# Expert gates with the heads innermost, and first-pass scores issued ahead of second-pass work

## The chip, the cores and the metric

The kernel runs on one core of a Trainium2 chip. The metric is the time of one execution on the device in microseconds, as the median of several runs. Each engine (TensorE, VectorE, ScalarE, GpSimd, SyncE) runs its own queue of instructions in order, and the kernel orders them against each other with semaphores.

## The reference

A stream x of shape (8, 512, 128) goes through four residual blocks: attention A, a mixture F, attention B, and the same F again. All are computed on a layer-normalised x.

```python
x = x + attn_a(layernorm(x))      # 16 heads of 8, rotary, causal softmax
x = x + ffn(layernorm(x))
x = x + attn_b(layernorm(x))      # the same shape, other weights and rotary table
x = x + ffn(layernorm(x))

def ffn(x):                       # H = 8 heads of 64, E = 5 experts, 2 chosen
    gl_v = (x @ Ws).reshape(b, t, h, e)
    wv = topk_mask(gl_v, 2) * sigmoid(gl_v)
    v = einsum('bthe,btek->bhtk', wv, einsum('btd,edk->btek', x, Wv))
    attn = softmax(q k^T * scale) @ v            # not causal, 512 x 512 per head
    mask_o = topk_mask((x @ Wd).reshape(b, t, h, e), 2)
    return einsum('bthe,bthk,ekd->btd', mask_o, attn, Wo)
```

What matters here: per token there are two sets of 8 x 5 gate logits. For each head the two largest of the five experts are kept, once with a sigmoid weight (for the values) and once as a plain mask (for the output).

## The kernel before

The work is 16 units (two rounds of 8 batch entries), each an attention block followed by a mixture block. The units are pipelined over iterations j of one long loop: iteration j prepares attention for unit j (`a_prep`), runs attention of unit j-1 (`a`) and prepares its mixture (`f_prep`), runs the mixture of unit j-2 (`f`) and ends that of unit j-3 (`f_end`). There are 19 iterations, and in iterations 3 to 15 all of this is active.

Each iteration has eight slots, 0 to 3 for the four head groups of attention and 4 to 7 for the four head pairs of the mixture, and each slot has ten steps b. Every engine walks the same grid of (slot, step) in its own queue, and the order inside a step is written out by hand.

For each head group there are two passes over the scores. `pass1` (L374) computes scores into one of three PSUM banks S1a to S1c, only so that VectorE finds the row maxima (`maxima`, L831) and, in the mixture, ScalarE takes the exponentials (`exps_f`, L677, into Pq). It runs two slots ahead: slots 2 to 5 hold the first pass of the mixture (L405, at even steps b = 0 to 6, two banks each), slots 6, 7, 0, 1 that of attention (L395 and L397, every step). `pass2` (L408) fills S2a and S2b: scores transposed again for attention (L423, slots 0 to 3), or transposes of Pq for the mixture (L429, slots 4 to 7). ScalarE moves them to PT (`exps`, L669 and L673), GpSimd masks them in attention (L1045), and `values` (L436, L455 and L464) multiplies PT of the slot before with the values into the bank Y. ScalarE copies Y to ySB at step 8 (L729) and TensorE transposes it in step 0 of the next slot (L490).

On TensorE (L598 on) each step issues pass2, then pass1, then values at odd steps, then what else stands in that step: the transposes of Z in step 9 of slot 1 (L582), the output projection of the mixture (L594), the gates (`f_gates`, L560) at steps 5 and 6 of slot 6, the mixture's Q/K projections (L557).

pass1 waits for `s1_free`, which is the reading of the bank three back: by VectorE's maximum in attention, by ScalarE's exponential in the mixture. Since the mixture's pass1 fills two banks at once, at step b it waits for the exponential of bank b-2. pass2 waits for `exps_done` of two banks back, and in the mixture for the exponentials of its own bank. ScalarE does in each step first `exps_f` of bank b-1 and then `exps` of bank b.

The choosing of experts is on VectorE. ScalarE copies the 80 gate logits of each of four token tiles from PSUM to `gate` (L717) in the order (tile, 16 = 8 + 8 heads, expert). `f_compare` (L884; L890 and L893) compares, for each expert e, its logit with those of the others, and writes 0 or 1 into `cmp_` in bfloat16, with the expert that does the beating innermost; nine instructions in steps 7 and 8 of slot 6. `f_count` (L899, L904) sums the innermost axis twice, half of the heads each, in step 9 of slot 6 and step 0 of slot 7: the number of experts that beat this one. `f_sigmoid` (L908) makes the sigmoid in slot 7, steps 1, 2 and 4, and the third step (L918) multiplies with (count < 1.5). `f_pick` (L923, L926) makes the output mask in step 5 of slot 1 of the next iteration. The value products (`f_value_product`, L930, L939) use wv_s from step 8 of slot 1 on, with GpSimd adding them up (L1069). `f_mix_weights` (L944) multiplies the mask with the reciprocal softmax sum into wz in step 1 of slot 6, and `f_mix` (L953, L965) multiplies y with wz, in steps 1 and 3 of slots 6, 7, 0 and 1, with GpSimd adding into Z (L1078) one step later.

## Time and profile before

| | |
|---|---|
| median of 3 runs | 2178.54 us (2177.8 to 2180.32) |
| the profiled execution | 2177.41 us, of which the span from first to last instruction is 2175.7 us |
| TensorE matmul busy | 1890.0 us (87%), 11328 instructions |
| VectorE busy | 1634.7 us (75%), 2950 instructions |
| ScalarE busy | 1278.2 us (59%), 2803 instructions |
| GpSimd busy | 1047.6 us (48%), 1124 instructions |
| mean granted TensorE clock | 0.947 of full speed |

A busy TensorE is a modelled figure, since matmuls are pipelined. Idle time is shown with its releaser: what ended the wait. The longest waits in total are GpSimd's for ScalarE's PT and for VectorE's products, and ScalarE's for the mixture's maxima; they say little, as these engines are not full. In the profile a slot is found by the transposes of ySB (L490), which stand in its step 0.

### The profile page before, as it was taken

The page shows a single profiled execution, that of the slowest core. Times are in us where ns is not written, and L with a number is a line of the kernel's source. Part 1 is how long each engine was busy: PE and PEld are TensorE (multiplying, and loading weights), DVE is VectorE, ACT ScalarE, POOL GpSimd, SP SyncE. Part 2 cuts the span into 40 slices and gives each one's busy share as a digit, 9 for nine tenths or more (in the row PEclk, how much of TensorE's full clock was granted, in tenths as well). Part 3 has the DMA queues.
Part 4 walks back from the last instruction along what each step waited for, and adds up shares of the span by engine and source line. Part 5 has one row for each costly group of instructions (what it writes and reads, how often), then busy time and mean ns, then how long its engine had stood idle before and what let it go on. Part 6 is the DMA issues. An engine that isn't in the chain of part 4 may idle for free.

```text
span 2175.7 us, 32651 instructions
## 1 busy us (share of the span) xinstructions
PE 1890.0 (87%) x11328; PEld 913.3 (42%) x11328; DVE 1634.7 (75%) x2950; ACT 1278.2 (59%) x2803; POOL 1047.6 (48%) x1124
## 2 busy tenths in 40 slices
PE   1658998999899999989999998999999899998775
PEld 0323544435354443535444353544435354443333
DVE  4548787978778797877879787787978788686561
ACT  0326657575665757566565756657575666657451
POOL 1215365463636556363655636365463646544433
PEclk8879999999999999999999999999999999999977
DMA  3221212020121202012120201212021121200000
GB/s 95 43 34 31 34 41 34 28 36 18 38 31 41 35 28 39 19 36 29 40 35 28 42 26 29 31 35 35 28 42 33 24 29 35 35 6 23 1 10 5
DMA packets 87617, 68.71 MB, mean 32 GB/s; under 512 B 10720, under 2 KB 83104, under 8 KB 87328
## 3 DMA queue, kind: packets, MB, share of 16 engines
q1 hardware_dynamic: 87456, 66.62, 16.3%
q8 instruction: 94, 1.54, 0.3%
q14 instruction: 67, 0.55, 0.1%
HBM read 32.51 MB, written 10.49 MB: 20 GB/s over the span
## 4 chain that ended last, share of the span: by engine, by line
PE 56%; DVE 30%; ACT 7%; issue 3%; DMA 2%; POOL 1%; SPq 0%; POOLq 0%; DVEq 0%; PEldq 0%; ACTq 0%
PE Y L464 8%; DVE nmaxF L849 5%; DVE nmaxA L844 5%; PE S1c L405 4%; PE S1b L405 4%; ACT Pq L684 4%; DVE ztmp L965 4%; PE S2a L429 4%; PE S2b L429 4%; PE M L594 3%; PE S1a L405 3%; PE Y L455 3%; PE M L557 3%; PE M L490 2%; DVE rotated L890 2%
## 5 line engine op out<-in xcount | busy, mean ns | idle before, releaser
L1078 POOL TENSOR_TENSOR Z<-Z,ztmp 128x1280 f32<-128x1280 f32 x112 | 324.5, 2898 | 353.3 <-DVE ztmp L965 351.2
L1045 POOL TENSOR_SCALAR_AFFINE_SELECT PT<-PT 128x256 f32<-128x256 f32 (+1 forms) x640 | 253.5, 406 | 372.8 <-ACT PT L669 368.9
L1069 POOL TENSOR_TENSOR Vf<-Vf,ztmp 128x512 f32<-128x512 f32 x256 | 349.6, 1366 | 146.8 <-DVE ztmp L939 138.3
L464 PE MATMUL Y<-PT,Vf 128*64 128x512 f32 x1024 | 274.8, 617 | 0.0
L669 ACT ACTIVATE PT<-S2a 128x512 f32<-128x512 f32 x320 | 191.3, 598 | 120.0 <-PE S2a L423 119.4
L405 PE MATMUL S1a<-Kf,Qf 64*128 64x512 f32 x352 | 217.5, 700 | 6.6 <-ACT Pq L684 4.6
L939 DVE TENSOR_TENSOR ztmp<-xv,wv_s 128x512 f32<-128x512 f32 x256 | 217.2, 848 | 2.8 <-POOL Z L1078 2.8
L405 PE MATMUL S1c<-Kf,Qf 64*128 64x512 f32 x352 | 207.9, 672 | 12.1 <-ACT Pq L684 10.8
L673 ACT ACTIVATE PT<-S2a 128x512 f32<-128x512 f32 x256 | 153.4, 599 | 89.2 <-PE S2a L429 89.0
L669 ACT ACTIVATE PT<-S2b 128x512 f32<-128x512 f32 x320 | 191.5, 598 | 16.3 <-PE S2b L423 15.7
L405 PE MATMUL S1b<-Kf,Qf 64*128 64x512 f32 x320 | 194.5, 690 | 6.5 <-ACT Pq L684 6.5
L849 DVE TENSOR_REDUCE nmaxF<-S1c 128x1 f32<-128x512 f32 x176 | 120.5, 685 | 93.9 <-PE S1a L405 93.9
L684 ACT ACTIVATE Pq<-S1c,nmaxF 128x512 f32<-128x512 f32 x176 | 121.6, 691 | 116.6 <-DVE nmaxF L849 116.6
L455 PE MATMUL Y<-PT,Vs 128*9 128x512 f32 (+3 forms) x2048 | 188.0, 441 | 0.0
L429 PE MATMUL S2a<-ident,Pq 128*128 128x128 f32 x1024 | 166.3, 285 | 24.0 <-ACT PT L669 24.0
L849 DVE TENSOR_REDUCE nmaxF<-S1a 128x1 f32<-128x512 f32 x176 | 120.4, 684 | 84.6 <-PE S1b L405 84.4
L965 DVE TENSOR_TENSOR ztmp<-M,wz 128x1280 f32<-128x1280 f32 x112 | 165.6, 1481 | 23.9 <-PE M L490 21.7
L429 PEld LDWEIGHTS S2a<-ident,Pq 128*128 128x128 f32 x1024 | 112.3, 142 | 161.6 <-ACT PT L673 88.3
L673 ACT ACTIVATE PT<-S2b 128x512 f32<-128x512 f32 x256 | 152.2, 595 | 30.0 <-PE S2b L429 27.6
L844 DVE TENSOR_REDUCE nmaxA<-S1b 128x1 f32<-128x128 f32 (+2 forms) x272 | 126.0, 492 | 54.5 <-PE S1b L397 54.5
L684 ACT ACTIVATE Pq<-S1a,nmaxF 128x512 f32<-128x512 f32 x176 | 121.0, 687 | 74.6 <-DVE nmaxF L849 74.5
L429 PE MATMUL S2b<-ident,Pq 128*128 128x128 f32 x1024 | 162.5, 283 | 0.0
(109 smaller groups left out, 3905.2 us busy)
## 6 DMA issues: line engine op xcount, KB each, us to landing
Qs<-parts SPq DMA_DIRECT2D x96, 128.0 KB
Ks<-parts SPq DMA_DIRECT2D x96, 128.0 KB
tab_s<-in_tab SPq DMA_DIRECT2D x16, 512.0 KB, 4.4
xr<-out_x SPq DMA_DIRECT2D x32, 256.0 KB, 2.9
out_x<-res SPq DMA_DIRECT2D x32, 256.0 KB, 2.2
wa_s<-in_wa SPq DMA_DIRECT2D x16, 320.0 KB, 3.1
xl<-out_x SPq DMA_DIRECT2D x16, 256.0 KB, 2.9
out_x<-in_x SPq DMA_DIRECT2D x8, 256.0 KB, 4.4
```

The source lines that it names most:

```text
L405: nc.tensor.matmul(S1[(n - 1 + h) % len(S1)][:, :], Qf[own, pair, qt * P:qt * P + P], Kf[own, pair, :], start=True, stop=True).then_inc(s1 ...
L429: last = nc.tensor.transpose(t[:, kt * P:kt * P + P], Pq[:, slot % 2, b, kt * P:kt * P + P], ident[:, :])
L455: last = nc.tensor.matmul(Y[32 * h:32 * h + DA + 1, kt * P:T], Vs[:, kt, GA * group + h, :], PT[:, group % 2, b, col:col + T - kt * P], st ...
L464: last = nc.tensor.matmul(Y[DF * h:DF * h + DF, :], Vf[:, kt, GF * (group - SA) + h, :], PT[:, group % 2, NT * h + kt, :], start=(kt == 0) ...
L669: nc.scalar.activation(PT[:, slot % 2, b, :], t[:, :], ACT.Exp, scale=SCALE_A).then_inc(exps_done.sem, 1)
L673: nc.scalar.activation(PT[:, slot % 2, NT * h:NT * h + NT, qt * P:qt * P + P], t[:, :].rearrange("p (k q) -> p k q", q=P), ACT.Copy).then_ ...
L684: nc.scalar.activation(Pq[:, g % 2, b, :], S1[(n - 1) % len(S1)][:, :], ACT.Exp, bias=nmaxF[:, GF * g + h, qt:qt + 1], accum_out=denF[:, G ...
L849: nc.vector.tensor_reduce(nmaxF[:, GF * (group - SA) + h, qt:qt + 1], t[:, :], AX.X, ALU.max, negate=True).then_inc(maxF_ready.sem, 1)
L965: nc.vector.tensor_tensor(ztmp[:, hh % 2, :, :, :] if hh else Z[:, :, :, :], y[:, :, h:h + 1, :].broadcast_to([P, NT, E, DF]), wz[:, :, hh ...
L1045: last = nc.gpsimd.affine_select(out=v, in_=v, compare_op=ALU.is_ge, fill=0.0, base=0, pattern=pattern, channel_multiplier=-1)
L1069: nc.gpsimd.tensor_tensor(Vf[:, i, :, :], Vf[:, i, :, :], vtmp[:, n % VBUF, :, :], ALU.add).then_inc(v_acc.sem, 1)
L1078: nc.gpsimd.tensor_tensor(Z[:, :, :, :], Z[:, :, :, :], ztmp[:, hh % 2, :, :, :], ALU.add).then_inc(z_acc.sem, 1)
```

## The change

Two things are changed. First, every array of the choosing has the experts outermost and the heads innermost. The columns of the gate weights are reordered on the host, `gate`, `beaten_by`, `wv_s` and `wz` become (expert, tile, head), `denF` and `recF` become (tile, head), and `cmp_` becomes (the beating expert, the beaten one, tile and head). The comparisons are then contiguous, and `f_count` reads its summed axis with a step of 320 bfloat16 elements. `f_pick` is removed with its array: `f_mix_weights` compares the count with 1.5 and multiplies in one scalar_tensor_tensor. The third sigmoid step goes from step 4 to step 9 of slot 7. Second, TensorE issues pass1 ahead of pass2 in each step.

```diff
@@ -125,20 +125,19 @@
         Kf = sb("Kf", [P, PAIRS, T])
 
         Pq = sb("Pq", [P, 2, GF * NT, T])
-        gate = sb("gate", [P, NT, 2 * HF, E])
+        gate = sb("gate", [P, E, NT, 2 * HF])
         xv = sb("xv", [P, NT, NX])
-        beaten_by = sb("beaten_by", [P, NT, 2 * HF, E], BF)
-        pick = sb("pick", [P, NT, HF, E])
-        wv_s = sb("wv_s", [P, NT, HF, E])
+        beaten_by = sb("beaten_by", [P, E, NT, 2 * HF], BF)
+        wv_s = sb("wv_s", [P, E, NT, HF])
         Vf = sb("Vf", [P, NT, HF, DF])
         nmaxF = sb("nmaxF", [P, HF, NT])
         rotated = sb("rotated", [P, 2, T])
         rot, rot2 = rotated[:, 0, :], rotated[:, 1, :]
         cmp_ = rotated[:, :, :].rearrange("p a t -> p (a t)").bitcast(BF)[:, 0:NT * 2 * HF * E * E].rearrange(
-            "p (g a b) -> p g a b", a=E, b=E)
-        denF = sb("denF", [P, HF, NT])
-        recF = sb("recF", [P, HF, NT])
-        wz = sb("wz", [P, NT, HF, E])
+            "p (b a g) -> p b a g", a=E, b=E)
+        denF = sb("denF", [P, NT, HF])
+        recF = sb("recF", [P, NT, HF])
+        wz = sb("wz", [P, E, NT, HF])
         Z = sb("Z", [P, NT, E, DF])
         ztmp = sb("ztmp", [P, 2, NT, E, DF])
         maskf = ztmp[:, 0, 0, 0:2, :].rearrange("p a b -> p (a b)")
@@ -234,7 +233,7 @@
         outA_chain = Signal("outA_chain", 1)
         maxA_chain = Signal("maxA_chain", SA)
         normA_chain = Signal("normA_chain", SA)
-        pick_chain = Signal("pick_chain", 7)
+        pick_chain = Signal("pick_chain", 6)
         mix_chain = Signal("mix_chain", 2)
 
         def bank(use):
@@ -597,10 +596,10 @@
 
                 for slot in range(NS):
                     for b in range(STEPS):
+                        if b < N_BANKS[(slot + AHEAD) % NS]:
+                            pass1(slot, b)
                         if b < N_BANKS[slot]:
                             pass2(slot, b)
-                        if b < N_BANKS[(slot + AHEAD) % NS]:
-                            pass1(slot, b)
                         if b % 2 == 1 and b < 2 * NT:
                             values(slot, b // 2)
                         at = (slot, b)
@@ -683,7 +682,7 @@
                         act.wait_ge(mix_chain.sem, mix_chain.at(j, 1, 3))
                     nc.scalar.activation(Pq[:, g % 2, b, :], S1[(n - 1) % len(S1)][:, :], ACT.Exp,
                                          bias=nmaxF[:, GF * g + h, qt:qt + 1],
-                                         accum_out=denF[:, GF * g + h, qt:qt + 1]).then_inc(expF_done.sem, 1)
+                                         accum_out=denF[:, qt, GF * g + h:GF * g + h + 1]).then_inc(expF_done.sem, 1)
 
                 def rows(group):
                     if not (a_prep if group == 0 else a):
@@ -714,7 +713,7 @@
                     if i == 0:
                         act.wait_ge(v_mult.sem, v_mult.at(j, v_mult.per, 2))
                     act.wait_ge(*filled(j, use))
-                    nc.scalar.activation(gate[:, i, :, :].rearrange("p g e -> p (g e)"), bank(use)[:, 0:NG], ACT.Copy)
+                    nc.scalar.activation(gate[:, :, i, :], bank(use)[:, 0:NG].rearrange("p (e g) -> p e g", e=E), ACT.Copy)
                     nc.scalar.activation(xv[:, i, :], bank(use)[:, NG:NG + NX], ACT.Copy).then_inc(is_free(use), 1)
 
                 for slot in range(NS):
@@ -761,8 +760,8 @@
                         if at == (6, 7) and f_prep:
                             act.wait_ge(*drained(j, "F gate2"))
                             act.wait_ge(*drained(j, "F gate3"))
-                            nc.scalar.activation(wv_s[:, :, :, :].rearrange("p t h e -> p t (h e)"),
-                                                 gate[:, :, 0:HF, :].rearrange("p t h e -> p t (h e)"),
+                            nc.scalar.activation(wv_s[:, :, :, :].rearrange("p e t h -> p (e t) h"),
+                                                 gate[:, :, :, 0:HF].rearrange("p e t h -> p (e t) h"),
                                                  ACT.Exp, scale=-1.0).then_inc(sig_e.sem, 1)
 
             for j in range(LAST):
@@ -885,28 +884,28 @@
                     if e == 0:
                         dve.wait_ge(*drained(j, "F gate2"))
                         dve.wait_ge(*drained(j, "F gate3"))
-                    gl = gate[:, :, :, :].rearrange("p t g e -> p (t g) e")
+                    gl = gate[:, :, :, :].rearrange("p e t g -> p e (t g)")
                     n_gl = NT * 2 * HF
-                    last = nc.vector.tensor_tensor(cmp_[:, :, 0:e + 1, e], gl[:, :, e:e + 1].broadcast_to([P, n_gl, e + 1]),
-                                                   gl[:, :, 0:e + 1], ALU.is_gt)
+                    last = nc.vector.tensor_tensor(cmp_[:, e, 0:e + 1, :], gl[:, e:e + 1, :].broadcast_to([P, e + 1, n_gl]),
+                                                   gl[:, 0:e + 1, :], ALU.is_gt)
                     if e < E - 1:
-                        last = nc.vector.tensor_tensor(cmp_[:, :, e + 1:E, e],
-                                                       gl[:, :, e:e + 1].broadcast_to([P, n_gl, E - 1 - e]),
-                                                       gl[:, :, e + 1:E], ALU.is_ge)
+                        last = nc.vector.tensor_tensor(cmp_[:, e, e + 1:E, :],
+                                                       gl[:, e:e + 1, :].broadcast_to([P, E - 1 - e, n_gl]),
+                                                       gl[:, e + 1:E, :], ALU.is_ge)
                     else:
                         last.then_inc(pick_chain.sem, 1)
 
                 def f_count(half):
                     dve.wait_ge(pick_chain.sem, pick_chain.at(j, 1, 1))
-                    n = NT * HF
-                    by = beaten_by[:, :, :, :].rearrange("p t g e -> p (t g) e")
+                    n = E * NT * HF
+                    by = beaten_by[:, :, :, :].rearrange("p e t g -> p (e t g)")
+                    beats = cmp_[:, :, :, :].rearrange("p b a g -> p (a g) b")
                     with nc.allow_low_precision(reason="counts of at most 4 are exact in bfloat16"):
-                        nc.vector.tensor_reduce(by[:, n * half:n * half + n, :], cmp_[:, n * half:n * half + n, :, :],
+                        nc.vector.tensor_reduce(by[:, n * half:n * half + n], beats[:, n * half:n * half + n, :],
                                                 AX.X, ALU.add).then_inc(pick_chain.sem, 1)
 
-
                 def f_sigmoid(step):
-                    wv2 = wv_s[:, :, :, :].rearrange("p t h e -> p (t h e)")
+                    wv2 = wv_s[:, :, :, :].rearrange("p e t h -> p (e t h)")
                     if step == 0:
                         dve.wait_ge(sig_e.sem, sig_e.at(j, 1, 1))
                         nc.vector.tensor_scalar(wv2, wv2, 1.0, None, ALU.add).then_inc(pick_chain.sem, 1)
@@ -915,21 +914,13 @@
                         nc.vector.reciprocal(wv2, wv2).then_inc(pick_chain.sem, 1)
                     if step == 2:
                         dve.wait_ge(pick_chain.sem, pick_chain.at(j, 5, 1))
-                        nc.vector.scalar_tensor_tensor(wv_s[:, :, :, :].rearrange("p t h e -> p t (h e)"),
-                                                       beaten_by[:, :, 0:HF, :].rearrange("p t h e -> p t (h e)"), 1.5,
-                                                       wv_s[:, :, :, :].rearrange("p t h e -> p t (h e)"),
+                        wv3 = wv_s[:, :, :, :].rearrange("p e t h -> p (e t) h")
+                        nc.vector.scalar_tensor_tensor(wv3, beaten_by[:, :, :, 0:HF].rearrange("p e t h -> p (e t) h"), 1.5, wv3,
                                                        ALU.is_lt, ALU.mult).then_inc(pick_chain.sem, 1)
-
-                def f_pick():
-
-                    dve.wait_ge(pick_chain.sem, pick_chain.at(j, 6, 2))
-                    nc.vector.tensor_scalar(pick[:, :, :, :].rearrange("p t h e -> p t (h e)"),
-                                            beaten_by[:, :, HF:2 * HF, :].rearrange("p t h e -> p t (h e)"), 1.5, None,
-                                            ALU.is_lt).then_inc(pick_chain.sem, 1)
 
                 def f_value_product(i, e):
                     if i == 0 and e == 0:
-                        dve.wait_ge(pick_chain.sem, pick_chain.at(j, 7, 2))
+                        dve.wait_ge(pick_chain.sem, pick_chain.at(j, 6, 2))
                         dve.wait_ge(y_filled.sem, y_filled.at(j, 1))
                     if i == 0 and e == 1:
                         dve.wait_ge(z_acc.sem, z_acc.at(j, HF - 1, 3))
@@ -939,16 +930,18 @@
                     nc.vector.tensor_tensor(
                         vtmp[:, n % VBUF, :, :] if e else Vf[:, i, :, :],
                         xv[:, i:i + 1, e * DF:(e + 1) * DF].broadcast_to([P, HF, DF]),
-                        wv_s[:, i, :, e:e + 1].broadcast_to([P, HF, DF]), ALU.mult).then_inc(v_mult.sem, 1)
+                        wv_s[:, e, i, :].unsqueeze(2).broadcast_to([P, HF, DF]), ALU.mult).then_inc(v_mult.sem, 1)
 
                 def f_mix_weights():
 
                     dve.wait_ge(expF_done.sem, expF_done.at(j, expF_done.per, 2))
                     nc.vector.reciprocal(recF[:, :, :], denF[:, :, :]).then_inc(mix_chain.sem, 1)
                     dve.wait_ge(mix_chain.sem, mix_chain.at(j, 1, 2))
-                    nc.vector.tensor_tensor(wz[:, :, :, :], pick[:, :, :, :],
-                                            recF[:, :, :].rearrange("p h t -> p t h").unsqueeze(3).broadcast_to([P, NT, HF, E]),
-                                            ALU.mult).then_inc(mix_chain.sem, 1)
+                    dve.wait_ge(pick_chain.sem, pick_chain.at(j, 3, 2))
+                    nc.vector.scalar_tensor_tensor(
+                        wz[:, :, :, :].rearrange("p e t h -> p e (t h)"), beaten_by[:, :, :, HF:2 * HF], 1.5,
+                        recF[:, :, :].rearrange("p t h -> p (t h)").unsqueeze(1).broadcast_to([P, E, NT * HF]),
+                        ALU.is_lt, ALU.mult).then_inc(mix_chain.sem, 1)
 
                 def f_mix(g, h, lag):
 
@@ -964,7 +957,7 @@
                         dve.wait_ge(z_acc.sem, z_acc.at(j, hh - 2, lag))
                     nc.vector.tensor_tensor(ztmp[:, hh % 2, :, :, :] if hh else Z[:, :, :, :],
                                             y[:, :, h:h + 1, :].broadcast_to([P, NT, E, DF]),
-                                            wz[:, :, hh, :].unsqueeze(3).broadcast_to([P, NT, E, DF]),
+                                            wz[:, :, :, hh].rearrange("p e t -> p t e").unsqueeze(3).broadcast_to([P, NT, E, DF]),
                                             ALU.mult).then_inc(z_mult.sem, 1)
                     if h == GF - 1:
                         dve.wait_ge(z_mult.sem, z_mult.at(j, GF * g + GF, lag))
@@ -1010,10 +1003,8 @@
                                 f_compare(e)
                         if at in ((6, 9), (7, 0)) and f_prep:
                             f_count(slot - 6)
-                        if at in ((7, 1), (7, 2), (7, 4)) and f_prep:
-                            f_sigmoid((1, 2, 4).index(b))
-                        if at == (1, 5) and f:
-                            f_pick()
+                        if at in ((7, 1), (7, 2), (7, 9)) and f_prep:
+                            f_sigmoid((1, 2, 9).index(b))
                         if at in V_STEPS and f:
                             f_value_product(*divmod(V_STEPS.index(at), E))
                         if at == (2, 1) and f_end:
@@ -1144,6 +1135,7 @@
     Wv, Wo = np.asarray(L0_ffn_Wv), np.asarray(L0_ffn_Wo)
     E, _, DH = Wv.shape
     HE = L0_ffn_Ws.shape[1]
+    gates = np.concatenate([np.asarray(w).reshape(C, HE // E, E) for w in (L0_ffn_Ws, L0_ffn_Wd)], 1)
     arrays = {
         "x": x,
         "wa": np.stack([a[0], b[0]]),
@@ -1153,7 +1145,7 @@
         "bp": np.stack([a[4], b[4]]),
         "tab": np.stack(tabs).astype(np.float32),
         "wqk": np.concatenate([np.asarray(L0_ffn_Wq), np.asarray(L0_ffn_Wk)], 1),
-        "wgv": np.concatenate([np.asarray(L0_ffn_Ws), np.asarray(L0_ffn_Wd), Wv.transpose(1, 0, 2).reshape(C, E * DH)], 1),
+        "wgv": np.concatenate([gates.transpose(0, 2, 1).reshape(C, 2 * HE), Wv.transpose(1, 0, 2).reshape(C, E * DH)], 1),
         "wo": Wo.reshape(E * DH, C),
         "ident": np.eye(128, dtype=np.float32),
         "mask": np.triu(np.full((128, 128), -1e30, np.float32), 1),
```

## Rows read from the trace of the kernel before

**Rows 1.** windows: span us, busy us (instructions) of PE, PEld, DVE, ACT, POOL, clock, DMA

```profile
1096.00:1222.00 126.00, 116.27 (x709) 56.47 (x708) 101.45 (x185) 79.52 (x175) 65.57 (x71) 0.97 0.16 33
```

**Rows 2.** VectorE groups by shape: count | busy us, mean ns | idle before

```profile
L844 DVE TENSOR_REDUCE nmaxA<-S1a 128x1 f32<-128x512 f32 x96 | 65.2, 680 | 3.1 <-PE S1a L397 3.1
L904 DVE TENSOR_REDUCE beaten_by<-rotated 128x160 bf16<-128x800 bf16 x32 | 31.1, 974 | 0.0
...
L844 DVE TENSOR_REDUCE nmaxA<-S1b 128x1 f32<-128x128 f32 x96 | 26.7, 278 | 0.0
L890 DVE TENSOR_TENSOR rotated<-gate 128x320 bf16<-128x320 f32 x16 | 20.5, 1281 | 0.0
L890 DVE TENSOR_TENSOR rotated<-gate 128x64 bf16<-128x64 f32 x16 | 7.1, 442 | 5.4 <-ACT xv L718 5.4
```

**Rows 3.** VectorE groups by line, shapes together

```profile
L890 DVE TENSOR_TENSOR rotated<-gate 128x64 bf16<-128x64 f32 (+4 forms) x80 | 69.6, 886 | 5.4 <-ACT xv L718 5.4
L893 DVE TENSOR_TENSOR rotated<-gate 128x256 bf16<-128x256 f32 (+1 forms) x64 | 54.5, 851 | 0.0
```

**Rows 4.** one line each: duration in ns as least/median/most

```profile
L918 DVE SCALAR_TENSOR_TENSOR wv_s<-beaten_by,wv_s x16: 319/2395/2405, 163.6 to 2036.1; 128x160 f32<-128x160 bf16 x16
L926 DVE TENSOR_SCALAR pick<-beaten_by x16: 234/2646/2659, 182.4 to 2051.2; 128x160 f32<-128x160 bf16 x16
```

**Rows 5.** TensorE timeline, slot 1: start us, duration us, what [idle before]

```profile
1186.59 0.39 PE L395 MATMUL S1c<-Ks,Qs 96*128 96x512 bf16 x1 [0.74 <-DVE nmaxA L839]
...
1190.41 0.28 PE L395 MATMUL S1b<-Ks,Qs 96*128 96x256 bf16 x1 [2.15 <-DVE nmaxA L844]
...
1190.76 2.69 PE L582 MATMUL M<-ident,Z 128*128 128x128 f32 x12
```

**Rows 6.** VectorE timeline, slot 1

```profile
1187.04 2.64 DVE L926 TENSOR_SCALAR pick<-beaten_by 128x160 f32<-128x160 bf16 x1
```

**Rows 7.** GpSimd timeline, slot 1

```profile
1186.71 2.88 POOL L1078 TENSOR_TENSOR Z<-Z,ztmp 128x1280 f32<-128x1280 f32 x1
```

**Rows 8.** windows, columns as in rows 1: behind slots 1 and 3, and slot 5

```profile
1191.00:1193.00 2.00, 2.00 (x11) 1.62 (x10) 1.93 (x10) 1.07 (x2) 1.17 (x2) 0.50 0.00 0
1193.00:1195.50 2.50, 2.50 (x11) 1.04 (x9) 2.50 (x7) 1.21 (x3) 1.28 (x3) 0.73 0.04 10
...
1228.00:1232.00 4.00, 4.00 (x18) 2.00 (x20) 2.02 (x5) 2.41 (x6) 2.08 (x4) 0.57 0.57 64
...
1241.00:1245.00 4.00, 2.78 (x24) 1.57 (x16) 4.00 (x6) 3.45 (x8) 3.23 (x3) 1.00 0.57 63
```

**Rows 9.** TensorE timeline, start of slot 3, inside it, start of slot 4

```profile
1211.99 0.38 PE L423 MATMUL S2a<-Qs,Ks 98*128 98x512 bf16 x1 [0.85 <-ACT PT L669]
...
1218.23 0.69 PE L405 MATMUL S1c<-Kf,Qf 64*128 64x512 f32 x1 [0.23 <-ACT Pq L684]
...
1219.29 1.98 PE L515 MATMUL M<-xnT,wa_s 128*128 128x512 f32 x4
...
1225.51 0.39 PE L423 MATMUL S2b<-Qs,Ks 98*128 98x256 bf16 x2 [1.09 <-ACT PT L669]
...
1227.56 0.66 PE L429 MATMUL S2a<-ident,Pq 128*128 128x128 f32 x4 [1.66 <-ACT PT L669]
```

**Rows 10.** ScalarE timeline, end of slot 3

```profile
1226.24 0.69 ACT L684 ACTIVATE Pq<-S1c,nmaxF 128x512 f32<-128x512 f32 x1 [0.79 <-DVE nmaxF L849]
...
1226.92 0.59 ACT L669 ACTIVATE PT<-S2a 128x512 f32<-128x512 f32 x1
```

**Rows 11.** TensorE timeline, starts of slots 5 and 6, and slot 7

```profile
1241.97 0.69 PE L405 MATMUL S1c<-Kf,Qf 64*128 64x512 f32 x1 [0.18 <-ACT Pq L684]
...
1244.13 0.66 PE L490 MATMUL M<-ident,ySB 128*128 128x128 f32 x4 [1.04 <-ACT ySB L729]
...
1259.91 0.66 PE L490 MATMUL M<-ident,ySB 128*128 128x128 f32 x4 [0.77 <-ACT ySB L729]
...
1288.22 1.98 PE L557 MATMUL M<-xnT,wqk_s 128*128 128x512 f32 x4 [0.73 <-DVEq L971]
```


## The prediction

> **What bounds the kernel now.** I read the busy time by stretches first. An iteration takes 126.15 us (the same stall stands at 1186.59 and 126.15 us later), and in 126 us of it TensorE is busy for 116.3 us and VectorE for 101.5 [rows 1]. TensorE is nearly full, so an edit is worth what it takes out of TensorE's 9.8 us of gaps, and what TensorE runs faster where a gap no longer lowers its clock. (The chain that ended last runs over TensorE and, in slots 6 to 1, over VectorE.) Then I walked TensorE's timeline through one iteration and noted each gap with its releaser: 0.74 and 2.15 us in slot 1 [rows 5], 0.85 before slot 3, 0.23 and 1.09 in slot 3, 1.66 before slot 4 [rows 9], 0.18 and 1.04 at the start of slot 5, 0.77 in slot 6, 0.73 in slot 7 [rows 11]. They add up to 9.4 of the 9.8 us. The clock comes last: granted 1.00 nearly everywhere, but 0.50 behind the slot 1 gaps and 0.57 behind the slot 3 gaps, while it stayed at 1.00 around the single gap of 1.04 us [rows 8]. Half speed is 1.2 of 2.4 GHz.
>
> **The change, part by part.** I go by iteration, and count the 15 in which attention and mixture both run (2 to 16).
>
> *The comparisons (f_compare).* Now 124.1 us in 16 iterations, 7.76 us each [rows 3]. They write and read across heads: from 64 to 320 elements the time grows by 839 ns, 3.3 ns an element, and 64 elements alone cost 442 ns [rows 2]. A contiguous reduction goes from 278 to 680 ns between 128 and 512 elements: 1.05 ns an element and 144 ns fixed [rows 2]. The nine new comparisons are contiguous: 1600 elements x 1.05 + 9 x 144 = 2.98 us, 4.8 us less on VectorE.
>
> *The counts (f_count).* Two reductions of 800 elements, 974 ns each [rows 2], whose innermost axis was contiguous and now steps by 640 bytes. The trace has no strided reduction. Lower end: 974 ns. Upper end: every element at the price of a comparison whose streams are all strided, (442 - 144) / 64 = 4.7 ns, so 800 x 4.7 + 144 = 3.9 us. I take 2.0 us, because only one stream of three is strided: +2.05 us for both, so choosing is 2.75 us shorter.
>
> The Trainium skill (SBUF, State Buffer; SBUF: two separate sides) speaks against this edit: lines are of 16 bytes, and each access that crosses to a new one pays. By it each count element would pay where five shared about one line; this trace shows the price in the comparisons only. What it would make of the time is the third rival below.
>
> *The pick (f_pick).* Removed. Its 16 instructions last 234 ns at best and 2646 ns at the median [rows 4]. In slot 1 it starts at 1187.04 and runs to 1189.68 [rows 6], and GpSimd's addition into Z runs from 1186.71 to 1189.59 [rows 7]: it ends when that ends. Its comparison moves into the wz instruction, where no GpSimd work runs, and I cost that at nothing (one 160-element instruction for another). Without it the sixth-step maxima of slot 1 start 2.6 us earlier, and TensorE doesn't wait 2.15 us at 1190.41. What is late next is GpSimd: the transposes of Z, at 1190.76, need the addition that ends at 1189.59 [rows 5, 7]. So the gain is 1190.76 - 1189.6 = 1.15 us, not 2.15, and a gap of about 1 us stays. The clock: at 0.50 for 2 us, and the next 2.5 us (0.73) still partly low [rows 8]; 1.0 + 0.7 us of work lost. One gap of 1 us is like the one that cost no clock, so I count 1.5 us back.
>
> The Trainium skill (SBUF, State Buffer; Who interferes with whom) gives the reason: VectorE and GpSimd share one port pair, and the later one is held until the other ends. The trace agrees (2646 against 234 ns).
>
> *The last sigmoid step.* 319 ns at best, 2395 at the median [rows 4], for the same reason; it moves from step 4 to step 9 of slot 7, behind five more maxima and away from the addition. Its readers, the value products, come in the last steps of slot 1. This saves 2.0 us of VectorE in slot 7, where TensorE only waits 0.73 us for VectorE, to free the bank for the third Q/K projection [rows 11]. The comparisons alone bring VectorE 2.75 us ahead of that point, so I count 0.7 us for all of slots 6 and 7; the rest is VectorE time that nobody waits for.
>
> *The order on TensorE.* Each step issued second pass, first pass, values, and will issue first pass, second pass, values. No DMA, SP or GpSimd queue is passed; the only thing moved is 1.06 us of F scores (at full clock, 1218.23 to 1219.29, four even steps of each of slots 2 to 5), or 0.3 to 0.4 us of A scores in slots 6 to 1. The two passes wait for different things: the first pass for a score bank that ScalarE's exponentials freed, the second pass for ScalarE's copy of two banks before. At the start of slot 4 TensorE waits 1.66 us for that copy, at 1226.92, which is itself behind the exponential of 1226.24 [rows 9, 10]. The first pass of that step needs only an older bank, so its 1.06 us go into the gap. At the start of slot 3 it fills the 0.85, but then the pass of step 4 comes to an exponential for which it already waits 0.23 us at 1218.23 [rows 9], and now 0.3 us of second pass are queued behind that wait; I let 0.5 of the 0.85 through. Sum 1.55 us. Behind slot 3 the clock is at 0.57 for 4 us, 1.7 us lost [rows 8]. There the gaps before were 1.09 and 1.66, and will be 1.09 and 0.6 with 1.4 us of work between. I leave the clock there as it is in the forecast, and keep the 1.5 us as a case.
>
> At the starts of slots 5 and 6 TensorE waits for ScalarE's copy of Y (1.04 and 0.77 us) [rows 11]; that copy stands behind the last exponential, thus behind the last first pass of the slot, which now comes one F second pass earlier (0.66 us as shown, 0.6 to its successor) [rows 9]. Slot 6: 0.6 us. Slot 5: 0.18 + 0.6, less 0.4 because in slot 4 the loop of first pass 1.06, second pass 0.6, its copy and the next exponential (0.59 and 0.69 [rows 10], some 0.2 more with hand-overs, an estimate) is 3.1 us, slightly more than TensorE's own work there. Left: 0.4 us.
>
> In slots 6 to 1 the first pass waits for VectorE's maxima of three banks before. Where VectorE is late (0.74 us at 1186.59) [rows 5], 0.3 us of second pass is now held behind it; it ends before GpSimd does, and costs nothing. If that cover were gone, 0.3 us an iteration.
>
> **Sum.** 1.15 + 1.5 (clock, slot 1) + 1.55 + 0.4 + 0.6 + 0.7 = 5.9 us a period, 15 x 5.9 = 88.5 us. The profiled execution took 2177.41 us (a span of 2175.7), 1.1 under the median 2178.54, which gives 2088.9 and 2090. The first and last iterations run other limits and I count nothing there.
>
> **Rivals.**
> 1. *Both low-clock stretches go*: 7.4 us a period, 2178.5 - 111 = 2067. For: four fifths of the stretch before slot 4 would be work. Against: the two gaps still add to 1.7 us.
> 2. *Neither goes*: 4.4 us, 2112.
> 3. *The counts by columns cost their upper end.* 3.9 us each is +5.85 on VectorE against the 4.8 saved, so the wait in slot 7 grows by 1.05 instead of losing 0.7: 4.15 us, 62 us, 2116. The rule of the Trainium skill on lines, above, points here.
> 4. *The order buys nothing*, as ScalarE and VectorE recur at their own pace and each early score only waits longer for its bank. Left are 1.15 + 1.5 + 0.7 = 3.35 us, 2128. For it: ScalarE waits for the maxima in these slots, 0.79 us in the row shown [rows 10].
> 5. *Slower.* The first pass blocks the second. In each of the 16 first-pass pairs of slots 2 to 5 TensorE stops for the exponential of two banks before, and the second pass, which could run in that wait, is issued behind it. Then the copies come late, and with them the next exponentials. If one attention second pass, 0.32 us, is lost at each, 5.1 us stand against the 3.35 of rival 4: +1.8 a period, 2205. It decides from 0.21 us a pair. Against it: only one of the pairs of slot 3 waits now, 0.23 us.
> 6. *No effect*: VectorE is only freed where TensorE was full. Against it speaks the slot 1 stall.
>
> **Chances.** Forecast 0.38, rival 1 0.18, rival 2 0.14, rival 3 0.10, rival 4 0.12, rival 5 0.06, rival 6 0.02. About 0.2% (4 us) is what a measurement of this kernel can tell from no change. Faster 0.92, within 0.2% 0.02, slower 0.06. The range runs from under rival 1 to over rival 4: 2055 to 2140.
>
> **What would show it.** No stall over 1.3 us in slot 1, its releaser GpSimd's Z addition and not VectorE; comparisons near 3 us an iteration; counts between 1 and 3.9 us; the last sigmoid step near 0.32 us; first-pass scores ahead of the gap at the start of slots 3 and 4; the copy of Y no longer waited for in slot 6. The forecast is wrong if TensorE's waits for the exponentials in slots 2 to 5 grow over 2 us a period, or if the clock behind slot 1 stays low.

## The result, and the profile after

The changed kernel takes 2077.8 us (median of 6, 2074.39 to 2081.19), the one before 2178.68 in the same comparison (2177.78 to 2180.32): ratio 0.9537, 95% interval 0.9524 to 0.9549. The forecast was 2090 in a range of 2055 to 2140, so sign and range held; the kernel gained 101 us where 88.5 were forecast. The profiled execution took 2074.39 us (span 2072.6). Line numbers (L...) from here on are those of the kernel named; the changed kernel's are 1 to 10 lower than before.

First the window of one iteration (columns as in [rows 1]):

```profile
1081.00:1200.00 119.00, 111.60 (x713) 54.40 (x712) 98.35 (x184) 79.50 (x176) 65.55 (x70) 1.00 0.20 34
```

The clock is 1.00 over the whole iteration (0.97 before), and TensorE is busy for 5 us less than in [rows 1] although it does the same work. Each execution has 13 iterations that are alike (counted from one first transpose of Z to the next). In the changed kernel ten of them keep the full clock, and three have one stretch of 3.4 us at half speed and last 1.4 to 1.6 us longer. Then TensorE's timeline through that iteration, the gaps alone:

```profile
1080.70 0.66 PE L489 MATMUL M<-ident,ySB 128*128 128x128 f32 x4 [0.73 <-ACT ySB L728]
...
1131.55 0.39 PE L394 MATMUL S1c<-Ks,Qs 96*128 96x512 bf16 x1 [0.21 <-DVE nmaxA L838]
1135.10 1.09 PE L581 MATMUL M<-ident,Z 128*128 128x128 f32 x8 [1.32 <-POOL Z L1069]
1136.50 0.63 PE L581 MATMUL M<-ident,Z 128*64 128x128 f32 x4 [0.31 <-ACT parts L659]
...
1146.91 0.69 PE L404 MATMUL S1a<-Kf,Qf 64*128 64x512 f32 x1 [0.34 <-ACT Pq L683]
1157.56 0.69 PE L404 MATMUL S1a<-Kf,Qf 64*128 64x512 f32 x1 [0.31 <-ACT Pq L683]
1161.25 0.69 PE L404 MATMUL S1c<-Kf,Qf 64*128 64x512 f32 x1 [1.26 <-ACT Pq L683]
1168.42 0.39 PE L422 MATMUL S2b<-Qs,Ks 98*128 98x256 bf16 x2 [0.76 <-ACT PT L668]
...
1170.37 0.66 PE L428 MATMUL S2a<-ident,Pq 128*128 128x128 f32 x4 [0.51 <-ACT PT L668]
1176.09 0.69 PE L404 MATMUL S1b<-Kf,Qf 64*128 64x512 f32 x1 [0.16 <-ACT Pq L683]
1179.16 0.69 PE L404 MATMUL S1a<-Kf,Qf 64*128 64x512 f32 x1 [0.37 <-ACT Pq L683]
1182.23 0.69 PE L404 MATMUL S1c<-Kf,Qf 64*128 64x512 f32 x1 [0.58 <-ACT Pq L683]
1184.14 0.66 PE L489 MATMUL M<-ident,ySB 128*128 128x128 f32 x4 [0.19 <-ACT ySB L728]
1199.49 0.66 PE L489 MATMUL M<-ident,ySB 128*128 128x128 f32 x4 [0.73 <-ACT ySB L728]
```

From the first to the last of these is one iteration, 118.79 us against 126.15: 7.4 us less. The gaps shown add to 7.05 us (9.4 before). Slot 1 waits 1.84 us (2.89 in [rows 5]), and the longest of its waits is for GpSimd's addition; the starts of slots 3 and 4 with what lies between, 2.84 (3.83 in [rows 9]); slot 5, 0.77 (1.22), slot 6 as before 0.73, slot 7 nothing [rows 11]. New waits: 0.34 in slot 2, 0.16 and 0.37 in slot 4.

Sorted by what they wait for, the waits of slots 2 to 5 moved more than they shrank. Those for ScalarE's exponentials (Pq) grew from 0.41 us (0.23 + 0.18) to 3.02; those for ScalarE's copies (PT and ySB) fell from 4.64 (0.85 + 1.09 + 1.66 + 1.04) to 1.46. Together that is 0.57 us less.

Behind slots 1 and 3 the clock stays up (the stretches of [rows 8]):

```profile
1135.50:1139.50 4.00, 3.69 (x26) 1.92 (x28) 3.96 (x12) 2.27 (x4) 2.47 (x6) 1.00 0.02 4
1170.50:1174.50 4.00, 3.96 (x28) 1.97 (x29) 3.57 (x7) 3.62 (x9) 3.37 (x5) 1.00 0.57 73
```

VectorE's groups by shape, against [rows 2 to 4]:

```profile
L904 DVE TENSOR_REDUCE beaten_by<-rotated 128x160 bf16<-128x800 bf16 x32 | 49.2, 1539 | 0.0
L889 DVE TENSOR_TENSOR rotated<-gate 128x320 bf16<-128x320 f32 x16 | 7.7, 481 | 0.0
...
L941 DVE SCALAR_TENSOR_TENSOR wz<-beaten_by,recF 128x160 f32<-128x160 bf16 x16 | 5.2, 325 | 0.5
L918 DVE SCALAR_TENSOR_TENSOR wv_s<-beaten_by,wv_s 128x160 f32<-128x160 bf16 x16 | 5.1, 316 | 0.1
...
L889 DVE TENSOR_TENSOR rotated<-gate 128x64 bf16<-128x64 f32 x16 | 3.4, 215 | 6.0 <-ACT xv L717 6.0
```

The nine comparisons sum to 3.01 us an iteration (forecast 2.98, before 7.76), the counts take 1539 ns each (forecast 2000, before 974), the last sigmoid step 316 ns.

### The profile page after: what moved, and what is told of

The parts are those of the page before. It is cut to its first block, busy times and chain, and to the rows that moved or that the text cites. A ratio compares the mean times of both kernels' runs of the same rounds, so it can differ in the third digit from the quotient of the medians.

```text
span 2072.6 us, 32651 instructions
## 1 busy us (share of the span) xinstructions
PE 1816.3 (88%) x11328; PEld 881.0 (43%) x11328; DVE 1580.1 (76%) x2934; ACT 1273.3 (61%) x2803; POOL 1047.0 (51%) x1124
## 4 chain that ended last, share of the span: by engine, by line
PE 64%; DVE 13%; ACT 10%; POOL 6%; DMA 3%; issue 3%; SPq 0%; POOLq 0%; DVEq 0%; ACTq 0%; PEldq 0%
PE Y L463 11%; PE M L556 5%; POOL Z L1069 5%; PE S2a L428 5%; ACT Pq L683 5%; PE S1c L404 5%; PE S2b L428 4%; DVE nmaxF L848 4%; PE M L593 3%; PE S1b L404 3%; PE M L514 3%; PE M L489 3%; DMA Ks<-parts 3%; DVE ztmp L930 3%; PE Y L454 2%
## 5 line engine op out<-in xcount | busy, mean ns | idle before, releaser
L930 DVE TENSOR_TENSOR ztmp<-xv,wv_s 128x512 f32<-128x512 f32 x256 | 238.0, 930 | 2.8 <-POOL Z L1069 2.8
L404 PE MATMUL S1c<-Kf,Qf 64*128 64x512 f32 x352 | 203.6, 659 | 36.2 <-ACT Pq L683 32.2
L404 PE MATMUL S1a<-Kf,Qf 64*128 64x512 f32 x352 | 204.5, 662 | 20.6 <-ACT Pq L683 20.6
L404 PE MATMUL S1b<-Kf,Qf 64*128 64x512 f32 x320 | 182.8, 652 | 9.5 <-ACT Pq L683 9.5
L428 PE MATMUL S2b<-ident,Pq 128*128 128x128 f32 x1024 | 155.3, 274 | 0.0
L848 DVE TENSOR_REDUCE nmaxF<-S1b 128x1 f32<-128x512 f32 x160 | 109.3, 683 | 40.0 <-PE S1c L404 37.9
```

What stands on the lines that cost most here:

```text
L404: nc.tensor.matmul(S1[(n - 1 + h) % len(S1)][:, :], Qf[own, pair, qt * P:qt * P + P], Kf[own, pair, :], start=True, stop=True).then_inc(s1 ...
L428: last = nc.tensor.transpose(t[:, kt * P:kt * P + P], Pq[:, slot % 2, b, kt * P:kt * P + P], ident[:, :])
L848: nc.vector.tensor_reduce(nmaxF[:, GF * (group - SA) + h, qt:qt + 1], t[:, :], AX.X, ALU.max, negate=True).then_inc(maxF_ready.sem, 1)
L930: nc.vector.tensor_tensor(vtmp[:, n % VBUF, :, :] if e else Vf[:, i, :, :], xv[:, i:i + 1, e * DF:(e + 1) * DF].broadcast_to([P, HF, DF]), ...
```

## The experiments

All ran in 3 rounds, each compared with runs of the kernel before on its own chip (2176.3 to 2179.5 us), so that ratios are comparable: changed kernel 0.9537.

### The two parts alone

e1_order_only is the kernel before with the new order; e2_layout_only is the changed kernel with the old order. The edit of e1 (that of e2 is the reverse):

```diff
-                        if b < N_BANKS[slot]:
-                            pass2(slot, b)
                         if b < N_BANKS[(slot + AHEAD) % NS]:
                             pass1(slot, b)
+                        if b < N_BANKS[slot]:
+                            pass2(slot, b)
```

> The kernel before with the first pass issued ahead of the second pass in every step; choosing, pick and sigmoid as before. Theory A (the prediction's sum, terms add): 1.55 + 0.4 + 0.6 us an iteration from the order and 1.5 from the clock behind slot 3, 4.05 x 15 = 61 us, about 2118 us (2140 if the low clock behind slot 3 stays). The 2.15 us stall of slot 1 and the 0.73 us wait in slot 7 stay. Theory B (only VectorE's relief counts; each early score waits longer for its bank): within 5 us of 2178. Theory C (the first pass holds up the second where VectorE is late, which only shows while the pick stands in slot 1): slower than 2178.

> The changed kernel with the second pass issued first again: only the heads innermost, no pick, sigmoid step in step 9. Theory A: 1.15 us (slot 1 up to GpSimd's addition) + 1.5 (clock behind slot 1) + 0.7 (slot 7) = 3.35 us x 15 = 50 us, about 2128 us; the gaps of 0.85, 1.09 and 1.66 us around slots 3 and 4 stay with the low clock behind them. Theory B: most of the 101 us, near 2080. If the two parts need each other, the gains of this run and of the order alone add to clearly less than 101 us; theory A says 111 with both clock terms.

Measured: e1 2091.06 us, ratio 0.9608 (0.9589 to 0.9628); e2 2121.14, ratio 0.9743 (0.9725 to 0.9761). The layout alone gained 55 us where 50 were expected; the order alone gained 85 where its theory A had 61. Together they gain 101 us, one by one 85 + 55 = 140, so 39 us are counted twice. By the traces these are, per iteration, 1.0 us of waits in slot 1 (2.89 before, 1.85 in e1, 1.92 in e2, 1.84 with both) and about 2.2 us of low clock: either part alone makes most of the low stretches go away. How the order removes the stall of slot 1 without touching the pick, VectorE's and GpSimd's timelines of e1 in slot 1 show:

```profile
1142.12 0.68 DVE L844 TENSOR_REDUCE nmaxA<-S1a 128x1 f32<-128x512 f32 x1
1142.72 0.28 DVE L926 TENSOR_SCALAR pick<-beaten_by 128x160 f32<-128x160 bf16 x1
1142.92 0.74 DVE L844 TENSOR_REDUCE nmaxA<-S1b 128x1 f32<-128x384 f32 x2
...
1142.87 2.89 POOL L1078 TENSOR_TENSOR Z<-Z,ztmp 128x1280 f32<-128x1280 f32 x1
```

In [rows 6, 7] the pick started 0.33 us behind GpSimd's addition and lasted to its end, 2.64 us. With the scores of each step issued one second pass earlier it starts 0.15 us ahead of the addition and takes 0.28 us. What e1 has against the changed kernel are two short waits for VectorE in slot 7, which stand behind the comparisons and counts:

```profile
1115.08 0.39 PE L395 MATMUL S1b<-Ks,Qs 96*128 96x512 bf16 x1 [0.20 <-DVE nmaxA L844]
1118.19 1.98 PE L557 MATMUL M<-xnT,wqk_s 128*128 128x512 f32 x4 [0.33 <-DVEq L971]
```

An iteration of e1 lasts 119.84 us, 1.05 more than the changed kernel's; the two waits are 0.53 of this. So on top of the order the layout is worth 1.05 us an iteration (forecast 0.7), and on top of the layout the order is worth 0.9743 - 0.9537, 45 us or 3.0 an iteration (forecast 2.55 without the clock behind slot 3, 4.05 with it).

### The pick moved instead of removed

e3_pick_moved is the kernel before with the pick at step 6 of slot 5 (two semaphore waits are moved to suit, not shown):

```diff
-                        if at == (1, 5) and f:
+                        if at == (5, 6) and f:
                             f_pick()
```

> The kernel before with one instruction moved: the pick goes from step 5 of slot 1 to step 6 of slot 5, where GpSimd has nothing to do. Theory A: the pick falls from 2646 to about 234 ns, the slot 1 stall of 2.15 us is replaced by a wait of about 1 us for GpSimd's Z addition, the clock behind it stays at 1.00: 2.65 us x 15 = 40 us, 2139 us. If the clock falls all the same: 1.15 x 15 = 17 us, 2161. Rival (the pick is slow by itself, because of its strided bfloat16 source): it stays near 2.6 us in its new place and the time stays within 10 us of 2178.

2159.34 us, ratio 0.9917 (0.9897 to 0.9938): 18 us, or 1.2 us an iteration, where 2.65 were forecast for this term. (The time is close to the 2161 that was expected if the clock behind slot 1 fell all the same, but that clock didn't fall; the match is luck.) The pick takes 233 ns, TensorE waits for GpSimd in slot 1, and the clock there is whole again. The forecast missed what happened elsewhere. Windows of e3 behind slot 1, behind slot 3 of that iteration, and behind slot 3 of the next:

```profile
1183.00:1187.00 4.00, 3.69 (x25) 1.87 (x27) 3.97 (x12) 2.16 (x4) 2.46 (x6) 1.00 0.02 6
1218.50:1222.50 4.00, 4.00 (x17) 2.01 (x16) 1.41 (x3) 2.35 (x6) 2.27 (x4) 0.57 0.57 68
...
1342.00:1347.00 5.00, 4.78 (x16) 2.79 (x16) 1.59 (x4) 2.92 (x7) 2.73 (x4) 0.50 0.57 74
```

Before, two stretches of 3.4 us ran at half speed in each iteration. In e3 the one behind slot 1 is gone, but the one behind slot 3 is 3.4 and 6.8 us long in turn. So in the mean only 1.7 us of low clock was saved, 0.85 us of time, and not 1.5. The gap fell by less than 1.15 as well: the waits of slot 1 in e3 are 0.74 + 1.07 + 0.31 = 2.12 us against 2.89.

### The pick put back under the addition

e9_order_pick_later is e1 with the pick one step later, where the addition is under way:

```diff
-                        if at == (1, 5) and f:
+                        if at == (1, 6) and f:
                             f_pick()
```

> The kernel with the new order alone (old layout, 2091.06 us), and the old pick of the five smallest moved from step 5 to step 6 of slot 1, where GpSimd's Z addition is under way. Theory A (the strided pick takes 233 to 285 ns when it runs ahead of GpSimd's addition and 2.6 us under it, and then holds up VectorE, then GpSimd and TensorE, as in the kernel before): pick at 2.6 us, the wait of some 1.15 us in slot 1 back, with or without 1.5 us of low clock behind it: 2108 to 2131. Rival B (what made the order alone so good has nothing to do with where the pick lies): 2087 to 2095.

2105.1 us, ratio 0.9662 (0.9648 to 0.9677), 0.86 us an iteration over e1 (120.70 against 119.84). Duration of the pick in ns as least/median/most, and TensorE behind it:

```profile
L926 DVE TENSOR_SCALAR pick<-beaten_by x16: 233/2478/2489, 185.1 to 1976.4; 128x160 f32<-128x160 bf16 x16
...
1152.25 0.66 PE L405 MATMUL S1c<-Kf,Qf 64*128 64x512 f32 x1 [0.81 <-DVE nmaxA L844]
```

So the place of the pick decides its length, as theory A says, but not its price: here 2.5 us of VectorE cost one wait of 0.81 us where theory A had at least 1.15, and the time lies between the two ranges, in neither. The end of the pick is the same each time: 0.10 us behind the end of the addition, whether it starts 0.34 us into it (the kernel before, 2.65 us long), 0.50 (e9, 2.48 us) or 1.53 (the last one of e1, 1.45 us). The Trainium skill (SBUF — State Buffer; SBUF: two separate sides) calls this an exclusive lock on one port pair, held for a whole instruction; 233 against 2478 ns for the same instruction agrees.

### One step of the order alone

e4_step0_only is the changed kernel with the scores first in step 0 of each slot and the second pass first elsewhere:

```diff
-                        if b < N_BANKS[(slot + AHEAD) % NS]:
+                        early = b == 0
+                        if early and b < N_BANKS[(slot + AHEAD) % NS]:
                             pass1(slot, b)
                         if b < N_BANKS[slot]:
                             pass2(slot, b)
+                        if not early and b < N_BANKS[(slot + AHEAD) % NS]:
+                            pass1(slot, b)
```

> The changed kernel with the first pass ahead of the second in step 0 of each slot only, and behind it in all other steps. Theory A: it keeps the filled gaps at the starts of slots 3 and 4 and the clock, and loses the 0.4 + 0.6 us an iteration that the earlier scores gave to the copies of Y at the starts of slots 5 and 6: about 15 us slower than the changed kernel, 2093. Rival: in the changed kernel TensorE waits 2.4 us an iteration for exponentials inside slots 3 and 4 (1.26, 0.15, 0.37, 0.58), with second-pass work queued behind; if that costs more than the earlier scores give, this kernel is faster than the changed one, 2065 or less.

2091.9 us, ratio 0.9606 (0.9587 to 0.9625). Step 0 alone carries two thirds of the order's gain (30 of 45 us). TensorE's timeline and the clock at the start of slot 4:

```profile
1178.20 0.39 PE L422 MATMUL S2b<-Qs,Ks 98*128 98x256 bf16 x2 [1.10 <-ACT PT L671]
1180.25 0.66 PE L428 MATMUL S2a<-ident,Pq 128*128 128x128 f32 x4 [0.60 <-ACT PT L671]
...
1180.50:1184.50 4.00, 4.00 (x29) 1.92 (x28) 3.15 (x5) 3.99 (x10) 3.37 (x5) 1.00 0.57 70
```

The 1.66 us of [rows 9] is 0.60, exactly as worked out, and with it the clock behind slot 3 stays at 1.00 in 10 of the 13 iterations that are alike. With 1.10 + 1.66 us it fell in all 13 of the kernel before and in 10 of e2; with 0.76 + 0.51 in one of the changed kernel and in none of e1. That is the clock term that the forecast left out.

The time of e4 is that of theory A, but not for its reason. It does lose 0.4 us at the start of slot 5 (1.21 us against 0.77), but 0.1 and not 0.6 at slot 6, and inside slots 2 to 4 it waits less; in all its waits are 6.73 us an iteration against 7.05. What makes it slower is something else, which the busy time of whole iterations at full clock shows (e2, e4, the changed kernel):

```profile
1162.37:1283.24 120.87, 112.96 (x709) 54.97 (x709) 96.11 (x184) 79.49 (x175) 65.45 (x71) 1.00 0.19 34
...
1144.59:1264.27 119.68, 112.81 (x708) 54.85 (x709) 96.86 (x184) 79.36 (x175) 65.65 (x71) 1.00 0.19 34
...
1016.31:1135.10 118.79, 111.39 (x708) 54.19 (x709) 98.21 (x184) 79.36 (x175) 65.55 (x71) 1.00 0.17 34
```

For the same matmuls TensorE is busy 1.4 to 1.6 us less when the scores come first in the steps behind step 0 too. The same for ten of the kernels; "own time" is an iteration at full clock less its waits of 0.15 us or more:

| kernel | scores first | iteration us | waits us | own time us | iterations with low clock, of 13 |
|---|---|---|---|---|---|
| before | no | 126.15 (clock low twice) | 9.47 | 113.3 (3.4 taken off for the clock) | 13 |
| e3 | no | 123.97 (clock low once) | 8.71 | 113.6 (1.7 taken off for the clock) | 13 |
| e2 | no | 120.87 | 7.77 | 113.1 | 10 |
| e4 | step 0 | 119.69 | 6.73 | 113.0 | 3 |
| e7 | all but 5 steps | 119.18 | 6.62 | 112.6 | 1 |
| e1 | all | 119.84 | 7.75 | 112.1 | 2 |
| changed | all | 118.79 | 7.05 | 111.7 | 3 |
| e5 | all | 118.30 | 6.57 | 111.7 | 0 |
| e10 | all | 117.44 | 5.71 | 111.7 | 2 |
| e12 | all | 116.90 | 5.19 | 111.7 | 0 |

So of the 3.0 us that the order is worth on top of the layout, 0.7 are waits, 1.4 are TensorE's own time and the rest is clock (10 low stretches against 3). Why the same matmuls take less in the new order was not tried.

### VectorE's time in slots 6 and 7

Two kernels add work into tiles that nobody reads. e8_twice does comparisons and counts a second time, e11_counts_twice the counts:

```diff
+                        nc.vector.tensor_reduce(by2[:, n * half:n * half + n], beats[:, n * half:n * half + n, :],
+                                                AX.X, ALU.add)
                         nc.vector.tensor_reduce(by[:, n * half:n * half + n], beats[:, n * half:n * half + n, :],
                                                 AX.X, ALU.add).then_inc(pick_chain.sem, 1)
...
+                                f_compare(e, cmp2, False)
                                 f_compare(e, cmp_, True)
```

> The changed kernel with the comparisons and the two counts each done a second time into tiles that nobody reads, 3.01 + 3.08 = 6.1 us more of VectorE an iteration in slots 6 and 7. The new layout saves about as much VectorE time there (7.76 + 1.95 before against 3.01 + 3.08 after: 3.6 us). Theory A (what the layout gives on top of the order is VectorE's time in slots 6 and 7, some 1.0 us an iteration, and a wait for VectorE at the start of slot 7 that comes back): the time goes up to that of the kernel with the new order alone or a little over, 2088 to 2105. Rival B (VectorE has room in these slots and what the layout gives lies elsewhere): 2076 to 2082.

> The changed kernel with the two counts alone done a second time into a tile that nobody reads: 3.1 us more of VectorE an iteration. With comparisons and counts doubled (6.1 us more) the time was 2156, and TensorE waited 0.88 + 1.42 + 1.19 + 0.33 = 3.8 us in slot 7 for VectorE's maxima, where it waits for nothing in the changed kernel. Theory A (VectorE has 6.1 - 3.8 = 2.3 us to spare in slots 6 and 7 in the changed kernel, and what goes past it costs its full time): 3.1 - 2.3 = 0.8 us an iteration, time 2086 to 2095; the same sum gives 3.6 - 2.3 = 1.3 us for the old layout's extra work, near to the 1.0 measured. Rival B (the cost grows in proportion from the first microsecond): half of 78 us, time 2113 to 2121.

e8: 2156.39 us, ratio 0.9898 (0.9883 to 0.9913). e11: 2124.48, ratio 0.9759 (0.9732 to 0.9787). Both fell outside both ranges, e11 only 3.5 us above rival B's: 6.1 us of VectorE cost 5.2 us an iteration, and 3.1 us of it cost 3.1, with a few more low stretches in both. TensorE in slot 7 of e11:

```profile
1128.85 0.28 PE L395 MATMUL S1a<-Ks,Qs 96*128 96x256 bf16 x1 [0.69 <-DVE nmaxA L844]
1130.99 0.39 PE L395 MATMUL S1b<-Ks,Qs 96*128 96x512 bf16 x1 [1.20 <-DVE nmaxA L844]
```

A third wait, of 0.33 us, stands at the Q/K projection, as in e1. So there is no common reserve of 2.3 us. At full clock an iteration of e11 lasts 121.53 us, 2.74 over the changed kernel, with 2.2 us of new waits for 3.1 us of VectorE; e8's lasts 123.28, 4.5 over it, with 3.8 us of new waits for 6.1. And a stop costs a little more than its gap: 0.5 us is not in the three new gaps of e11 and 0.7 not in the four of e8, some 0.17 us a stop. The likely reason is that matmuls overlap (the profile starts one of 0.22 us 0.06 us ahead of its successor) and a stop lays the end of the last one open; that was not tried by itself.

The third step of the sigmoid, back at step 4 of slot 7 (e6_sigmoid_back):

```diff
-                        if at in ((7, 1), (7, 2), (7, 9)) and f_prep:
-                            f_sigmoid((1, 2, 9).index(b))
+                        if at in ((7, 1), (7, 2), (7, 4)) and f_prep:
+                            f_sigmoid((1, 2, 4).index(b))
```

> The changed kernel with the third step of the sigmoid (L918) put back from step 9 to step 4 of slot 7, as in the kernel before, where it lies beside a Z addition of GpSimd. Theory A (a strided operation of VectorE beside GpSimd's addition takes 2.4 us instead of 0.32; in slot 7 of the changed kernel it takes what VectorE has to spare there, 2.3 us, so most of it is not seen): L918 at 2.4 us, time 2074 to 2085. Rival B (every microsecond of VectorE in slot 7 is paid): 2.1 us times 15, time 2105 to 2112.

2081.2 us, ratio 0.9558 (0.9531 to 0.9584), not distinct from the changed kernel, with the step at full length:

```profile
L918 DVE SCALAR_TENSOR_TENSOR wv_s<-beaten_by,wv_s x16: 314/2401/2405, 164.0 to 1938.4; 128x160 f32<-128x160 bf16 x16
```

So moving this step gives nothing that can be measured (an iteration at full clock lasts 118.82 us against 118.79): 2.1 us at step 4 are free, where 3.1 us at steps 9 and 0 are not. The gain of the layout on top of the order therefore lies elsewhere. The shorter comparisons are the likely place, as e1's two waits come right behind them; no run takes them apart from the removed pick.

### The waits that are left

e7_hybrid issues the second pass first at five steps of slots 2 to 4, to work inside the waits for ScalarE:

```diff
+                        early = (slot, b) not in ((2, 2), (3, 2), (3, 4), (4, 4), (4, 6))
```

> The changed kernel, but at five steps (second and third step pairs of slots 2 to 4, where TensorE still waits for exponentials or copies behind the scores: 0.34, 0.31, 1.26, 0.76, 0.51 us an iteration) the second pass is issued first again. Theory A (the waits that are left are for the banks of the first pass, and second-pass work done inside them fills them): about 1.8 us an iteration less, 15 times, time 2051 to 2060. Rival B (ScalarE's and VectorE's work comes at its own pace, so a wait filled at one step comes back at the next, and the old order brings its own waits of 0.8 to 1.1 us back): 2078 to 2095.

2080.6 us, ratio 0.9553 (0.9538 to 0.9569): the time is in rival B's range. The 1.26 us of slot 3 came back as waits of 0.81 and 0.28, the 0.58 at the start of slot 5 as 0.76 and its 0.19 as 0.45. In all the waits fell by 0.4 us an iteration, and TensorE's own time grew by 0.8 (table above), which is not what either theory says. Order alone gains nothing more here. The next three kernels, each on top of the one before, take away what ends such a wait last. e5_z_first issues GpSimd's addition ahead of the mask:

```diff
+                        if b in (2, 4) and slot in (0, 1, 6, 7) and (f if slot > 1 else f_end):
+                            f_mix((slot - 2) % NS - SA, b // 2 - 1, 3 if slot < 2 else 2)
                         if slot < SA and a:
                             mask(slot, b)
```

> The changed kernel with GpSimd's additions for the mix of the values issued ahead of that step's mask instead of behind it. In the changed kernel TensorE waits 1.32 us in slot 1 (L581 at 1135.10), for the Z addition that started at 1132.15 and took 2.89 us. Theory A (the addition is late because GpSimd issues it late): the addition starts up to 0.76 us earlier (two masks), the wait shrinks by as much, 15 iterations times 0.76 gives up to 11 us, time 2067 to 2072. Rival B: the addition doesn't start earlier, as it waits for VectorE's product, or the masks that it holds up delay the values by as much: 2076 to 2082, with a wait for the masks in its place.

e10_product_later moves one value product of VectorE:

```diff
-        V_STEPS = [ ... (3, (0, 2, 4, 7)), ...
+        V_STEPS = [ ... (3, (1, 2, 4, 7)), ...
```

> The kernel with GpSimd's Z addition ahead of the mask (2067 us), and one value product of VectorE moved from step 0 to step 1 of slot 3. In slot 3 TensorE waits 1.26 us for ScalarE's copies of the scores, which in turn waited 1.27 us for a maximum that VectorE did at 1154.64, behind a value product of 1.52 us and the reciprocal and product of the norm (0.24 and 0.29 us). Theory A (the pile of VectorE's work at step 0 of slot 3 is what ends that wait last): the wait falls by some 0.7 us, up to 10 us less, time 2055 to 2062. Rival B (the product brings the same wait one step later, or the waits behind it, 0.76 and 0.51 us for exponentials, grow): 2064 to 2072.

The wait for ScalarE's copy of Y at the start of slot 6 is left in all of these. ScalarE ahead of this copy, in the changed kernel (first and last of a row without a pause: copy, exponential, copy, exponential, copy of Y):

```profile
1196.53 0.60 ACT L672 ACTIVATE PT<-S2a 128x512 f32<-128x512 f32 x1 [1.39 <-PE S2a L428]
...
1198.82 0.61 ACT L728 ACTIVATE ySB<-Y 128x512 f32<-128x512 f32 x1
```

The first of them waited for TensorE's second pass, which the new order issues behind the scores. e12_transposes_later moves the transposes of Y of slot 6:

```diff
-                        if b == 0:
+                        if b == (1 if slot == 6 else 0):
                             value_transposes(slot)
```

> The kernel with GpSimd's addition first and the value product moved (2058.55 us), and the transposes of Y at the start of slot 6 issued one step later, behind the first value product of step 1. They are where TensorE waits for ScalarE's copy of Y, 0.73 us an iteration in the changed kernel and in both kernels derived from it (the prediction had this wait go with the new order, which it didn't do). Theory A (the copy comes 1.6 us after the last product of the values, and a step of scores and second-pass work between the two covers it): the wait goes, 0.7 us an iteration, time 2046 to 2052. Rival B (the exponential of this step then takes TensorE's wait over, as ScalarE does the copy in front of it, or VectorE's mix, which reads the transposes, comes later and holds up the maxima of slot 6): 2055 to 2064.

The times are in theory A's range each time. e5: 2067.32 us, ratio 0.9485 (0.9470 to 0.9499), the wait in slot 1 down from 1.32 to 0.74. e10: 2058.55, ratio 0.9454 (0.9430 to 0.9477); VectorE in slot 3 of e5, and TensorE's wait there in e10 (1.26 us in e5):

```profile
1152.11 0.68 DVE L848 TENSOR_REDUCE nmaxF<-S1b 128x1 f32<-128x512 f32 x1
1152.71 1.52 DVE L930 TENSOR_TENSOR ztmp<-xv,wv_s 128x512 f32<-128x512 f32 x1
1154.16 0.24 DVE L868 RECIPROCAL recA<-M 128x16 f32<-128x16 f32 x1
1154.43 0.29 DVE L870 TENSOR_TENSOR yN<-M,recA 128x128 f32<-128x128 f32 x1
1154.64 0.68 DVE L848 TENSOR_REDUCE nmaxF<-S1c 128x1 f32<-128x512 f32 x1
```

```profile
1153.41 0.69 PE L404 MATMUL S1c<-Kf,Qf 64*128 64x512 f32 x1 [0.38 <-ACT Pq L683]
```

e12: 2046.96, ratio 0.9396 (0.9381 to 0.9411), an iteration of 116.90 us; the transposes no longer wait, and a wait of 0.22 us for VectorE comes up behind them:

```profile
1183.21 1.08 PE L463 MATMUL Y<-PT,Vf 128*64 128x512 f32 x4
1184.22 0.66 PE L489 MATMUL M<-ident,ySB 128*128 128x128 f32 x4
```

At full clock the three edits take 0.49, 0.86 and 0.54 us off an iteration. The medians fell by more after e5 (10.5 us, where 15 x 0.49 = 7.4), because its 13 iterations lost the three low stretches, which nothing in the edit aimed at. e12 beats the kernel before by 6.0% and the changed kernel by 1.5%.

## Why the prediction was right, and where its terms were off

Per iteration, forecast and measured (the iteration shown above, against one of the kernel before):

| term | forecast us | measured us | from |
|---|---|---|---|
| wait in slot 1 | 1.15 | 1.05 | 2.89 to 1.84 |
| clock | 1.5 | 3.4 | two stretches of 3.4 us at half speed, both gone; 3.0 in the mean of 13 |
| starts of slots 3 and 4 | 1.55 | 0.99 | 3.83 to 2.84 |
| new waits in slots 2 and 4 | 0 | -0.87 | 0.34, 0.16, 0.37 |
| slot 5 | 0.4 | 0.45 | 1.22 to 0.77 |
| slot 6 | 0.6 | 0.0 | 0.77 to 0.73 |
| slot 7 | 0.7 | 0.7 | 0.73 to 0 |
| TensorE's own time | 0 | 1.6 | the rest of 7.4 |
| sum | 5.9 | 7.4 | |

The direction, the bound and the parts of the layout were right. That the number came out so near is partly luck: the order's waits were put 1.9 us too high (2.55 forecast, 0.6 measured) and the clock 1.9 us too low, and these two cancel. The gain above the forecast is then TensorE's own time, a term that the sum does not have.

- *What bounds the kernel*: right. TensorE stayed the bound, but what was won is gaps, clock and 1.6 us of its own time.
- *The pick and what is late next*: right in releaser, and near in size. The step "not 2.15 but 1.15, as GpSimd's addition ends 1 us before" was to leave 1.0 us behind the 2.15; 1.63 are left (1.32 for that addition, 0.31 for a copy of ScalarE), and the other 0.5 us of the term came from the 0.74, now 0.21, which was not forecast. e5 shows that GpSimd's own queue held the addition for 0.6 us.
- *The clock* was mis-sized. Behind slot 3 it was forecast to fall all the same; e4 shows it at 1.00 in 10 of 13 iterations once the second gap is 0.60 instead of 1.66. Rival 1's 7.4 us an iteration is the measured 7.4 only by the same cancelling of terms. Over the 13 iterations that are alike the mean gain is 7.0 us, as three of them keep a low stretch; that makes 91 us, and some 10 more came from the first and last iterations, where nothing was counted. And the term "clock behind slot 1, 1.5" doesn't stand by itself: e3 removes that stretch and gets half of it back behind slot 3.
- *Slots 3 and 4*: the start of slot 4 went as worked out (e4: 1.66 to 0.60). But most of the old waits moved on rather than vanished. The prediction named its own sign of failing, waits for exponentials in slots 2 to 5 that grow by more than 2 us: they grew by 2.6 (0.41 to 3.02). For the waits alone rival 4 was therefore closer: 2.55 us were forecast from the order in slots 2 to 6, none by rival 4, and 0.6 came. The order paid all the same, through the clock, slot 1 and TensorE's own time. The 1.26 us in slot 3 was not seen, because its cause (a value product, two norm instructions and a maximum in a row on VectorE) was hidden behind the old order; e10 shows that cause.
- *Slot 6*: the step failed. The prediction had the copy of Y come earlier with the last exponential. But in the changed kernel the row of ScalarE work that ends with this copy begins with a copy of the scores, and that one waits 1.39 us for the second pass, which is now issued behind the scores. e12 takes the 0.73 us by a move of the transposes.
- *TensorE's own time*, put at nothing: 1.6 us an iteration. It comes with the order, mostly in the steps behind step 0 (e4); its cause stays open.
- *Comparisons, counts*: 3.01 for 2.98, and 1539 ns for 2000, in the bounds of 974 and 3900. By the line rule that stood behind rival 3 (the Trainium skill, SBUF — State Buffer; SBUF: two separate sides) every count element crosses to a new line; (1539 - 144) / 800 = 1.7 ns an element, against 1.05 contiguous and 4.7 in the old comparisons, so here the penalty is real but small.
- *The last sigmoid step, costed at nothing*: right (e6). The remark that the rest of VectorE's time in slots 6 and 7 is waited for by nobody was wrong at the counts: in e11 an iteration at full clock pays 2.7 us for 3.1.
- *Overlap of the parts*: the prediction gave the stall in slot 1 to the layout alone. It was right for the sum, but the order removes it too (e1), by an alignment that the trace of before could have hinted at: the pick was only 0.33 us late.
- *Slower (rival 5)* needed 0.21 us lost at each of 16 pairs. The waits for exponentials grew by 2.6 us, 0.16 a pair, but the waits for copies fell by 3.2.

## What to carry to other kernels

Price a stall by what is late next, and add the clock of the stretch behind it, but take the clock over the whole iteration: a removed dip may lengthen the next one. A VectorE instruction like the pick has no fixed length beside one of GpSimd: a start 0.5 us later made it nine times as long. So look for such pairs ahead of moving or deleting anything. A wait whose releaser stands at the end of a row of other work was removed or shortened here by moving that work or the waiting instruction one step (e5, e10, e12), not by a new order of the passes on the engine that waits (e7). And when a sum comes out, compare it term by term: here two errors of 1.9 us cancelled, and a third term was missing.

## What the runs showed of the hardware

- The pick took 233 to 285 ns away from or just ahead of GpSimd's addition (e3, e1) and 2.5 to 2.65 us started 0.5 or 0.34 us into it (e9, before); it ended 0.10 us behind the addition each time. L918 took 0.32 us alone and 2.40 beside the addition (changed kernel, e6).
- The low clock comes in stretches of 3.4 us, or 6.8, at 0.50. It fell behind gaps of 0.74 and 2.15 us in every iteration that is alike (before), behind 1.10 and 1.66 in all 13 of the kernel before and 10 of 13 in e2, behind 1.10 and 0.60 in 3 of 13 (e4), behind 1.32 and 0.31 in 2 of 13 and behind 0.76 and 0.51 in 1 of 13 (changed kernel). What tells the iterations of one kernel apart is open.
- A reduction of 800 bfloat16 elements with its innermost step at 640 bytes took 1539 ns, contiguous 974. Comparisons along contiguous heads took 1.04 ns an element and 148 ns.
- New stops of TensorE cost about 0.17 us each beyond the gap that the timeline shows (e8, e11).
- The order in which the same matmuls are issued changed TensorE's own time by 1.4 us in an iteration (113.1 us in e2, 111.7 in the changed kernel).
